# Shared expert of a gated attention and mixture-of-experts block, taken apart from the mixing: 12 of 32 token tiles run before the expert slots, 20 behind them

## The reference

```python
def _L0_ffn_ref(hidden_states, w_router, w_gate, w_up, w_down, ws_gate, ws_up, ws_down):
    ...                                     # E = 8 experts, TOP_K = 2, F = 176, FS = 352, SCALE = 2.5
    probs = jax.nn.softmax(x @ w_router, axis=-1)
    top_v, top_i = jax.lax.top_k(probs, TOP_K)
    top_v = top_v / jnp.sum(top_v, axis=-1, keepdims=True)
    combine = jnp.zeros((T, E), x.dtype).at[jnp.arange(T)[:, None], top_i].set(top_v)
    g = jax.nn.silu(jnp.einsum('td,edf->etf', x, w_gate))
    u = jnp.einsum('td,edf->etf', x, w_up)
    y = jnp.einsum('etf,efd->etd', g * u, w_down)
    routed = jnp.einsum('etd,te->td', y, combine) * SCALE
    shared = jax.nn.silu(x @ ws_gate) * (x @ ws_up) @ ws_down
    return (routed + shared).reshape(B, S, D)
...
x = x + jnp.tanh(g_xattn[0]) * _L0_xattn_ref(_layernorm(x, axis=-1), ctx_2048, ...)
x = x + jnp.tanh(g_ffn[0]) * _L0_ffn_ref(_layernorm(x, axis=-1), ...)
```

## Time and profile before

| | |
|---|---|
| Time, median of 3 runs | 1428.82 us (1428.08 to 1429.32) |
| Profiled execution, span from its first to its last instruction | 1426.6 us |
| What lies around that span: median less span | 2.2 us |
| Busy, share of the span | PE 90%, DVE 80%, ACT 62%, POOL 64% |
| Attention | 0 to 1081 us |
| Gap, up to the first gate and up of a slot | 1081 to 1125.2 us |
| Slots | 1125.2 to about 1299 us |
| Shared expert and mixing | 1298.8 to 1426.6 us |

### The profile page before, as it was taken

How to read it: one execution, slowest core, us unless ns; L and a number is a source line. 1 busy time by engine, 2 the same in 40 slices (tenths; PEclk the granted TensorE clock), 3 DMA queues, 4 the chain that set the end, 5 groups by cost and what they waited for, 6 DMA issues and landing times.

```text
span 1426.6 us, 31847 instructions
## 1 busy us (share of the span) xinstructions
PE 1277.5 (90%) x8826; PEld 1159.4 (81%) x8827; DVE 1142.0 (80%) x3159; ACT 880.8 (62%) x3737; POOL 919.8 (64%) x1097
## 2 busy tenths in 40 slices
PE   0599999999999999999999999999995499999997
PEld 0488888888888888888888888888884388889896
DVE  8778888888888888888888888888885766665665
ACT  4667776777676767767676767676774355553221
POOL 6677777777777777777777777777773200003665
PEclk9799999999999999999999999999996699999998
DMA  6403211111111111111111111111103233334775
GB/s 191 133 5 134 106 58 41 35 35 35 35 38 39 42 51 39 35 35 35 39 37 37 49 48 35 35 35 35 39 27 118 68 111 110 110 110 136 207 222 172
...
## 3 DMA queue, kind: packets, MB, share of 16 engines
...
## 4 chain that ended last, share of the span: by engine, by line
PE 33%; DVE 26%; POOL 17%; issue 14%; ACT 8%; DMA 1%; POOLq 0%; DVEq 0%; SPq 0%; ACTq 0%
PE b_kv L1470 7%; PE b_o L1521 4%; ACT probs L770 3%; POOL qk_r L575 3%; POOL q_rot L579 3%; PE b_q L1647 3%; PE b_kv L1647 3%; DVE q_sin L1038 3%; DVE row_max L1048 3%; POOL k_rot L588 3%; DVE k_rot L1022 2%; PE b_sc L1495 2%; POOL xs_scratch L601 2%; POOL sin_w L559 2%; DVE k_sin L1024 2%
## 5 line engine op out<-in xcount | busy, mean ns | idle before, releaser
L770 ACT ACTIVATE probs<-b_sc,neg_max 128x128 f32<-128x128 f32 x512 | 180.9, 369 | 44.4 <-DVE neg_max L1051 44.4
L1470 PE MATMUL b_kv<-wkv_hi,kv_in_hi 128*128 128x256 f32 x512 | 163.9, 320 | 42.9 <-DVE k_sin L1024 42.9
L575 POOL TENSOR_TENSOR qk_r<-qk_me,minus_half 128x6 f32<-128x6 f32 x128 | 171.1, 1337 | 10.0
L579 POOL TENSOR_TENSOR q_rot<-q_rot,q_sin 128x512 f32<-128x512 f32 x128 | 164.4, 1285 | 0.0
L1521 PE MATMUL b_o<-wo_hi,aT_hi 128*128 128x256 f32 x512 | 155.6, 304 | 1.4 <-DVE aT_lo L1064 1.4
L1470 PEld LDWEIGHTS b_kv<-wkv_hi,kv_in_hi 128*128 128x128 f32 x512 | 98.0, 191 | 69.4 <-DVE k_sin L1024 67.5
L1470 PE MATMUL b_kv<-wkv_lo,kv_in_hi 128*128 128x256 f32 x512 | 145.4, 284 | 0.0
L1470 PE MATMUL b_kv<-wkv_hi,kv_in_lo 128*128 128x256 f32 x512 | 145.1, 283 | 0.0
L1521 PE MATMUL b_o<-wo_hi,aT_lo 128*128 128x256 f32 x512 | 144.4, 282 | 0.0
L1521 PE MATMUL b_o<-wo_lo,aT_hi 128*128 128x256 f32 x512 | 144.4, 282 | 0.0
L1456 PE MATMUL b_q<-wq_hi,kv_in_hi 128*128 128x512 f32 x256 | 113.3, 443 | 30.7 <-DVE kv_in_lo L1011 29.3
...
## 6 DMA issues: line engine op xcount, KB each, us to landing
...
trig_raw<-trig_scratch SPq DMA_DIRECT2D x128, 32.0 KB
```

The lines of the kernel that those rows point to most:

```text
L575: nc.gpsimd.tensor_tensor(qk_r[g % 2][:], qk_me[:], minus_half[:, 0:REP + NB], ALU.pow).then_inc(r_ready, 1)
L579: nc.gpsimd.tensor_tensor(q_rot[g % 2][:], q_rot[g % 2][:], q_sin[g % 2][:], ALU.add) \
L770: last = nc.scalar.activation(probs[:, j, :], b_sc[:, j * P:(j + 1) * P], ACT.Exp, bias=neg_max[g % 2][:, j:j + 1], scale=SCALE, accum_out ...
L1470: last = nc.tensor.matmul(b_kv[:, s * 2 * HD:(s + 1) * 2 * HD], kv_in[p][a][:, c, 2 * s:2 * s + 2, :], wkv_s[b][:, c, g % KVH, :], start=( ...
```

## The change

The shared expert is taken out of the mixing and becomes a step that adds into x1.

- x1 of all 32 tiles is loaded into one buffer on chip, `x1_all` (32 KB per partition). It lies where the output weights `wo` of the attention lay, so SP loads its first 24 tiles (one DMA of 3072 KB) behind a wait for the last `b_o` matmul, and the last 8 (1024 KB) once the last x1 is stored. `add_shared(t)` on DVE adds gate times the shared output of tile t to it in place.
- Tiles 0 to 11 of the shared expert run in the gap, one piece at a time between the steps of the last tile's routing and of the table, on PE, ACT and DVE. Tiles 12 to 31 run behind the slots, with no loop.
- Their split tokens come from a ring of 8 buffers `yS`, which SP loads. Gate, up, transposes and down have one PSUM bank each (`banks`); silu waits for gate only, hidden for up.
- The mixing is 32 mixes of two sums each, in the order `MIX_ORDER`: 0, 12, 1, 13, 2, and so on. `mixes(t)` tells how many stand behind each late tile: none behind tiles 12 and 13, then 7 in 5 tiles, and 7 are left behind tile 31. POOL's gathers take their indices straight from `at_all`, have a ring of 4 and lose the three small instructions; mix m waits for its two gathers, and gather m for the mix m - 4.
- The weights of the shared expert stand first in the order of splitting (`W2_ORDER`).

```diff
+EARLY = 12
+RING = 8
+ROUTED_RING = 4
...
+        x1_all = sb("x1_all", [P, TILES, D], F32, wo_at)
...
-        b_gate, b_up, b_hT, b_y = [b_q, b_kv], [b_qT, b_kT], b_sc, [b_aT, b_o]
+        b_early, b_late = (b_q, b_kv, b_qT, b_sc), (b_q, b_sc, b_pT, b_aT)
...
+        SHARED_G, SHARED_D = (8, 9), 4
+        W2_ORDER = [("g", n) for n in SHARED_G] + [("d", SHARED_D)] + [("g", n) for n in range(4)]
+        for n in range(4):
+            W2_ORDER += [("d", n)] + [("g", m) for m in range(4 + 2 * n, min(6 + 2 * n, 8))]
+
+        first_late = [t for t in range(EARLY, TILES)]
+        MIX_ORDER = [t for pair in zip(range(EARLY), first_late) for t in pair] + first_late[EARLY:]
+
+        def banks(t):
+            gate, up, hT_bank, y = b_early if t < EARLY else b_late
+            return gate, up, hT_bank, b_o if 6 <= t < EARLY else y
+
+        def mixes(t):
+
+            def by(j):
+                return min(TILES, max(0, (7 * j - 15) // 5))
+
+            j = t - EARLY
+            return range(by(j), TILES if t == TILES else by(j + 1))
...
+            def load_yS(t):
+                i, r = divmod(t, RING // 2)
+                if t >= RING:
+                    sp.wait_ge(up_done, t - RING + 1)
+                elif t >= RING // 2:
+                    sp.wait_ge(q_done, 4 * TILES)
+                    sp.wait_ge(kv_done, 4 * TILES)
+                need(sp, ld_yS[r], 16 * i)
+                sp.wait_ge(st_yT, 16 * (t + 1))
+                sp.dma_start(yS_both[t % RING][:].rearrange("p a c n -> p (a c n)").bitcast(F32),
+                             yT_dram[t, :, :]).then_inc(ld_yS[r], 16)
+
+            X1_SPLIT = 24
+
+            def load_x1(q):
+                some = (slice(0, X1_SPLIT), slice(X1_SPLIT, TILES))[q]
+                sp.dma_start(x1_all[:, some, :], x1_dram[some, :, :].rearrange("t p n -> p t n")).then_inc(ld_x1[q], 16)
...
+            for t in range(RING // 2, RING):
+                load_yS(t)
...
+            sp.wait_ge(o_done, 4 * TILES)
+            for p in range(2):
+                sp.wait_ge(st_x1[p], 16 * (PAIRS - 1))
+            load_x1(0)
             store_x1(TILES - 1, 1)
             store_yT(TILES - 1, 1)
-
-
-            sp.wait_ge(table_ready, 1)
+            for p in range(2):
+                sp.wait_ge(st_x1[p], 16 * PAIRS)
+            load_x1(1)
+            for t in range(RING, 2 * RING):
+                load_yS(t)
+
+            sp.wait_ge(tables_ready, 2)
             sp.wait_ge(st_xs, 16 * TOPK * TILES)
...
             load_slot(0, 0)
             load_slot(1, 1)
+            for t in range(2 * RING, EARLY + RING):
+                load_yS(t)
...
+            def store_out(m):
+                sp.wait_ge(out_ready, m + 1)
+                sp.dma_start(out[MIX_ORDER[m], :, :], o_out[m % 2][:]).then_inc(st_out[m % 2], 16)
+
+            for t in range(EARLY + RING, TILES):
+                load_yS(t)
+                for m in mixes(t - RING):
+                    store_out(m)
+            for t in range(TILES - RING, TILES + 1):
+                for m in mixes(t):
+                    store_out(m)
...
+            def gather(m):
+                r, t = m % ROUTED_RING, MIX_ORDER[m]
+                if m >= ROUTED_RING:
+                    pool.wait_ge(out_ready, m - ROUTED_RING + 1)
                 for j in range(TOPK):
-                    nc.gpsimd.indirect_dma_start(out=routed[p][j][:], out_offset=None, in_=ys_dram[:, :],
-                                                 in_offset=bass.IndirectOffsetOnAxis(ap=at_t[p][:, j:j + 1], axis=0)) \
-                      .then_inc(ld_routed[p], 16)
...
+            silu_gate(0)
+            hidden_hi(0)
             probs_out(4 * TILES - 1, 3)
             split2_hi(1)
+            silu_gate(1)
             attended_hi(4 * TILES - 1, 3)
-            split2_hi(3)
+            hidden_hi(1)
+            split2_hi(1)
+            silu_gate(2)
+            split2_hi(1)
+            hidden_hi(2)
+            silu_gate(3)
             tokens_hi(TILES - 1, 1)
+            split2_hi(1)
+            hidden_hi(3)
+            silu_gate(4)
             split2_hi(2)
+            hidden_hi(4)
+            silu_gate(5)
             lead_tanh(TILES - 1)
-            split2_hi(len(W2_ORDER) - 10)
-            nc.scalar.activation(gates_raw[:, 0:1], gates[:, 0:1], ACT.Silu)
...
+            hidden_hi(5)
+            for t in range(6, EARLY):
+                if t < 10:
+                    split2_hi(1)
+                silu_gate(t)
+                hidden_hi(t)
 
...
+            def hidden(t):
+                dve.wait_ge(silu_done, t + 1)
+                dve.wait_ge(up_done, t + 1)
+                need(dve, hT_done, t - 1)
+                nc.vector.tensor_tensor(hid[t % 2][:, 0:FS], silu[t % 2][:], banks(t)[1][:, 0:FS], ALU.mult) \
+                  .then_inc(hid_ready, 1)
+
+            def hidden_lo(t):
+                dve.wait_ge(hT_hi, t + 1)
+                nc.vector.tensor_tensor(hT[LO][:].rearrange("p c n -> p (c n)"), banks(t)[2][:, 0:FW],
+                                        hT[HI][:].rearrange("p c n -> p (c n)").bitcast(F32), ALU.subtract) \
+                  .then_inc(hT_lo, 1)
+
+            def add_shared(t):
+
+                dve.wait_ge(y_done, t + 1)
+                dve.wait_ge(ld_x1[t // 24], 16)
+                nc.vector.scalar_tensor_tensor(out=x1_all[:, t, :], in0=banks(t)[3][:, 0:D], scalar=gates[:, 1:2],
+                                               in1=x1_all[:, t, :], op0=ALU.mult, op1=ALU.add).then_inc(shared_ready, 1)
+
+            def first_sum(m):
+
+                r, t = m % ROUTED_RING, MIX_ORDER[m]
+                dve.wait_ge(ld_routed[r], 16 * TOPK * (m // ROUTED_RING + 1))
+                dve.wait_ge(shared_ready, t + 1)
+                nc.vector.scalar_tensor_tensor(out=x1_all[:, t, :], in0=routed[r][0][:], scalar=w_all[:, t, 0:1],
+                                               in1=x1_all[:, t, :], op0=ALU.mult, op1=ALU.add).then_inc(mix_step, 1)
+
+            def second_sum(m):
+
+                r, t = m % ROUTED_RING, MIX_ORDER[m]
+                dve.wait_ge(mix_step, m + 1)
+                need(dve, st_out[m % 2], 16 * (m // 2))
+                nc.vector.scalar_tensor_tensor(out=o_out[m % 2][:], in0=routed[r][1][:], scalar=w_all[:, t, 1:2],
+                                               in1=x1_all[:, t, :], op0=ALU.mult, op1=ALU.add).then_inc(out_ready, 1)
...
             T2, T1 = TILES - 2, TILES - 1
+            hidden(0)
             weights_and_mask(T2)
+            hidden_lo(0)
             read_ranks(T2)
             rows_of_tokens(T2, 0)
+            hidden(1)
+            split2_lo(1)
             attended_lo(4 * TILES - 1, 3)
-            split2_lo(1)
+            hidden_lo(1)
+            hidden(2)
             residual(T1, PAIRS - 1, 1)
             layer_stats2(T1, 1)
             dve.wait_ge(stats2, TILES)
             layer_var2()
+            add_shared(0)
+            add_shared(1)
+            hidden_lo(2)
+            hidden(3)
+            normalize_y(T1, 1)
             split2_lo(1)
-            normalize_y(T1, 1)
+            add_shared(2)
             tokens_lo(T1, 1)
-            split2_lo(1)
+            hidden_lo(3)
+            hidden(4)
+            add_shared(3)
             copy_logits(T1)
             dve.wait_ge(lg_copied, TILES)
...
+            for t in range(9, EARLY):
+                split2_lo(1)
+                hidden(t)
+                add_shared(t - 1)
+                hidden_lo(t)
+            split2_lo(1)
+            add_shared(EARLY - 1)
             for p in range(2):
...
+            for t in range(EARLY, TILES):
+                hidden(t)
+                if t > EARLY:
+                    add_shared(t - 1)
+                hidden_lo(t)
+                for m in mixes(t):
+                    first_sum(m)
+                    second_sum(m)
+            add_shared(TILES - 1)
+            for m in mixes(TILES):
+                first_sum(m)
+                second_sum(m)
...
+            def shared_gate_up(t):
+
+                r, shared = t % RING, banks(t)
+                pe.wait_ge(ld_yS[t % (RING // 2)], 16 * (t // (RING // 2) + 1))
+                need(pe, silu_done, t)
+                for j, done in enumerate((gate_done, up_done)):
+                    if j == 1:
+                        need(pe, hid_ready, t)
+                    for c in range(DC):
+                        for a, b in PASSES:
+                            last = nc.tensor.matmul(shared[j][:, 0:FS], yS[r][a][:, c, :], wg_s[b][:, c, j * FS:(j + 1) * FS],
+                                                    start=(c == 0 and (a, b) == PASSES[0]),
+                                                    stop=(c == DC - 1 and (a, b) == PASSES[-1]))
+                    last.then_inc(done, 1)
+
...
+            def shared_down(t):
+                pe.wait_ge(hT_lo, t + 1)
+                need(pe, shared_ready, t)
...
```

(31 more changed lines are left out.)

320 lines of the change are left out of this document (126 added, 194 removed).

## The result

| | us, median (lowest to highest) | runs |
|---|---|---|
| before, beside it | 1429.07 (1428.08 to 1430.01) | 4 |
| changed | 1442.18 (1440.25 to 1447.35) | 4 |
| ratio | 1.0099, 95% interval 1.008 to 1.0118 | |
| predicted | 1422.0, range 1406 to 1440 | |

The changed kernel is 1% slower, and the forecast was 20 us too low. The expectations, written while this came to light, call them the fast and the slow condition.

What follows compares the result with a forecast made beforehand. It took the gap to be bound by DVE's routing and table chain, the last stage by PE's tiles plus gathers. Span 1426.6 + 28.5 (gap) - 35.3 (last stage) = 1419.8, with 2.2 around it 1422.0 us; range 1406 to 1440.

Steps and rivals of the forecast that it cites:

- Up to the last slot: Attention's end to the last slot: gap grows by 28.5 us, first slot at 1154.5, slots themselves unchanged.
- The clock's case: Rival, gap between x1's arrival and first slot: PE stays at the lower clock, 16 us more, 1438 us; chance 0.16.
- The last stage: Stage behind the slots: 64 gathers at 1.28 us on POOL bound it, 92.5 us, 35.3 less than 127.8.
- the prediction's second bound: Last stage: ring on DVE of hidden, transposes, splits and mixes, about 3.7 us a tile, just inside the gathers' pace.
- The term: Last stage's length, bound by POOL's gathers: 92.5 us, bounds 88 to 99.
- the sum: Whole kernel: 1426.6 + 28.5 - 35.3 = 1419.8 us of span, 1422.0 us with the 2.2 around it.
- The fourth rival: Last stage: sums on VectorE stretch each of 64 gathers by 0.2 us, 1435 us; chance 0.07.

Runs made afterwards that it cites:

- set 1: First group of runs, alternated on one chip: changed kernel against the kernel before; 1442.2 us against 1429.1.
- e17: Changed kernel with 9 instead of 12 early tiles, x1's load cut at tile 8, eight pairs of routed rows; 1451.2 us, ratio 1.0163 to before.
- e13: Changed kernel with only the first 8 of its 64 gathers, sums rereading the same rows; 1417.1 us.
- e19: Changed kernel with three small integer additions on GpSimd between every two gathers; 1447.3 us.
- e5: Changed kernel unchanged, measured again; 1422.7 us, ratio 0.9962 to the kernel before.
- e9: Changed kernel unchanged, measured a third time as a control; 1445.7 us.
- e1: Kernel before with its last stage written out in full on all five engines instead of a loop; 1429.2 us, ratio 1.0006.
- sets 3 and 4: Two groups of runs on the same chip, each with the changed kernel unchanged; 1422.7 us in the former, 1445.7 in the latter.
- e10: Changed kernel with x1's load cut at tile 8 instead of tile 24; 1441.3 us against 1445.7 for the unchanged control.
- e12: Same program as e17, against the kernel before in an earlier group of runs; 1411.0 us, ratio 0.9888.

## Why the prediction was wrong

- **Up to the last slot: right within 2 us, in part by offsets.** The last attention matmul ended at 1093.2 instead of 1096 (1091.8 to 1097.0 in the later traces), with a granted clock of 0.88 from 1081 to 1095, where the earlier trace rows has 0.59. From there x1's 3072 KB took 11.3 us instead of 11, VectorE waited 10 us, and from x1's arrival to the first slot it was 48.4 us instead of 47.5. The last stage starts 26.7 us later than before; the prediction had 28.5 (its own terms give 28.3: 1154.5 less 1125.2, less 1).
- **The clock's case did not come:** granted clock 1.00 at 1110 to 1125.
- **The last stage: the step that failed.** The prediction put it: "So POOL is the bound, PE has slack, and the stage takes 92.5 us". It priced the gathers' move from about 1.8 us apart (64 in 115 us) to 1.28 at nothing but GpSimd's own time. In set 1, and in four of the seven others, gathers that close go with late signals of TensorE, up to 4.5 us here and 17.7 in e17; from 2 us behind the last gather of e13 on, or at 1.73 us apart (e19), they are on time. The late signals fall on TensorE's one-tile chain, gate, `hid`, transposes, `hT_hi`, `hT_lo`, down, whose single banks leave nothing to do meanwhile. This chain is the prediction's second bound, the ring of "about 3.7 us a tile, 74 us for 20". It took 74.0 us in e5 and 97.9 us here, and so bound the stage in GpSimd's place: GpSimd waited 25.8 us for its sums. Part of the loss is the clock, which fell behind some of the pauses: up to the end of tile 31 it was granted 0.86 here and 1.00 in e5 (columns of the earlier trace rows):

```profile
1325.45:1423.34 97.89, 80.95 (x486) 77.13 (x485) 52.20 (x111) 19.66 (x42) 52.61 (x55) 0.86 0.47 141
...
1328.46:1402.48 74.02, 69.32 (x486) 67.39 (x485) 51.77 (x111) 19.89 (x42) 51.64 (x53) 1.00 0.62 181
```

  The term was 22 us short; the late starts of `hT_hi` alone add up to 14.0.
- **Where the signals are on time the sum was right:** 1422.7 against 1422.0, ratio 0.9962, POOL's 1.28 us a gather, 93.3 against 92.5 us, the span of the trace 1421.8 against 1419.8. That the sets differ was not foreseen, and the change's own set was not of this kind.
- **The fourth rival named the right partner and the wrong victim.** It had gathers stretched by the sums. The median gather takes 0.946 us in set 1 and in e5 alike; its gathers were never slower, TensorE's signals were. The Trainium skill (TensorE: Matmul & The Clock Gate, "The cost: per-tile semaphore tail") prices the increments of a semaphore that follow one another, one by each matmul of a packed array, at about 26 ns each. By that figure four increments a token tile would be about 0.1 us, an estimate; no run here has packed matmuls, and the 4.5 us of e9 are not of this size, nor are they a cost of increments: where signals are on time, `hT_hi` starts 0.04 us behind the transposes with the same four.
- **What stood in the trace of before.** Nine starts of `hT_hi` 0.50 to 0.71 us late, and 14 whose releaser the waits don't name; in e1, without late signals, they name TensorE 31 times and nothing else. The 14 are on time, 0.04 us behind the transposes: what is missing is the record of the rise. Waits of before, and of e1, 1300 to 1424 us:

```profile
ACT hT_hi L945 <- PE b_sc L1727: 25.6, 17, 2.2
ACT hT_hi L945 <- issue: 19.8, 14, 2.6
```

```profile
ACT hT_hi L946 <- PE b_sc L1728: 40.3, 31, 2.7
```

There the loop was bound by gathers and lost nothing by it that shows: before took 1426.8 to 1429.1 in the five sets with late signals and 1427.1 to 1428.5 in the three without. I had read that slack as room, and it was also a cushion.

Open: what makes a set one or the other. It is not the chip alone (sets 3 and 4 shared one), not the program, and it stays for all runs of a set. Where the backlog stands, in the signals' way or in TensorE, the traces don't show. In sets with late signals only the gathers' number and pace were varied (and the load of x1, the ring and the early tiles in e10 and e17), so another cause that acts together with them is not excluded. One rival stands untested. Every time on record comes with the core's span and clock, so it is of an execution that was recorded, and the traces with late signals are the ones that lack records while gathers run. The recording itself may have a part in the delay; no run without it is there to tell.

No version tried here is faster than before in both conditions: e12 is 1.1% faster than before without late signals and e17, the same program, 1.6% slower with them. The kernel before, whose gathers are further apart, is within 2.4 us in all eight.
